# First attention takes one batch's rows through DRAM ahead of its main block, and five stages end with a square root on ScalarE

## The reference, cut to what matters

```python
def _layernorm(x, axis=-1, eps=1e-05):
    m = jnp.mean(x, axis=axis, keepdims=True)
    v = jnp.var(x, axis=axis, keepdims=True)
    return (x - m) / jnp.sqrt(v + eps)
...
xn = _layernorm(x, axis=-1)
x = x + _L0_attn_ref(xn, ...) + _L0_ffn_ref(xn, ...)
xn = _layernorm(x, axis=-1)
x = x + _L1_attn_ref(xn, ...) + _L1_ffn_ref(xn, ...)
...
```

```python
q = (x @ Wq + bq).reshape(b, h, dh, t)
k = (x @ Wk + bk).reshape(b, h, dh, t)
v = (x @ Wv + bv).reshape(b, h, dh, t)
attn = jnp.einsum('bhdt,bhds->bhts', k, v) * temperature
attn = jax.nn.softmax(attn, axis=-1)
out = jnp.einsum('bhdt,bhts->bhds', q, attn)
```

## Time and profile before

| | |
|---|---|
| runs, median (lowest to highest) | 2434.83 us (2428.15 to 2442.73), 3 runs |
| profiled execution, its time | 2452.63 us |
| its span in the trace | 2451.0 us |
| mean granted TensorE clock | 0.884 |
| PE busy | 2014.1 us (82%) |
| DVE busy | 1738.9 us (71%) |
| ACT busy | 1195.2 us (49%) |
| POOL busy | 536.9 us (22%) |

### The profile page before, as it was taken

How to read it: one execution, slowest core, us unless ns; L and a number is a source line. 1 busy time by engine, 2 the same in 40 slices (tenths; PEclk the granted TensorE clock), 3 DMA queues, 4 the chain that set the end, 5 groups by cost and what they waited for, 6 DMA issues and landing times. The chain is left out here.

```text
span 2451.0 us, 45364 instructions
## 1 busy us (share of the span) xinstructions
PE 2014.1 (82%) x17632; PEld 1041.8 (43%) x17632; DVE 1738.9 (71%) x2865; ACT 1195.2 (49%) x2429; POOL 536.9 (22%) x640
## 2 busy tenths in 40 slices
PE   1788876965739999899789879988799798797898
PEld 1222222632302339633343248845544345555554
DVE  3899998667789885598554963355666697866665
ACT  2899998233408772488533223324443021075433
POOL 1112110014954431244402521125300000001100
PEclk8798999976659999899877889978899899988899
DMA  7423420001723226333100122201123423000000
GB/s 253 80 53 80 77 53 1 1 17 45 193 79 102 51 53 202 82 70 46 19 10 16 38 69 89 94 28 36 44 66 92 155 77 98 5 6 25 1 0 35
DMA packets 146772, 155.89 MB, mean 64 GB/s; under 512 B 53004, under 2 KB 122314, under 8 KB 146562
## 3 DMA queue, kind: packets, MB, share of 16 engines
q1 hardware_dynamic: 131912, 119.78, 18.9%
q0 software_dynamic: 12928, 25.47, 4.0%
q10 hardware_dynamic: 1728, 7.87, 0.8%
HBM read 87.37 MB, written 68.55 MB: 64 GB/s over the span
## 5 line engine op out<-in xcount | busy, mean ns | idle before, releaser
L427 ACT ACTIVATE a_E<-a_scores,a_nmax 128x512 f32<-128x512 f32 x512 | 343.6, 816 | 11.7 <-DVE a_nmax L360 11.4
L999 ACT ACTIVATE a_E<-a_scores 128x512 f32<-128x512 f32 x512 | 272.8, 601 | 115.5 <-PE a_scores L1032 105.2
L902 DVE TENSOR_REDUCE a_nmax<-a_first 128x2 f32<-128x1024 f32 x256 | 297.0, 1218 | 27.4 <-PE a_first L1022 25.1
L360 DVE TENSOR_REDUCE a_nmax<-a_scores 128x2 f32<-128x1024 f32 x256 | 302.6, 1218 | 18.4 <-PE a_scores L442 14.2
L442 PE MATMUL a_scores<-a_Vh,a_Kh 48*128 48x512 bf16 x512 | 107.7, 419 | 100.7 <-ACT a_E L427 71.6
L1032 PE MATMUL a_scores<-a_Qh,a_Kh 51*128 51x512 bf16 x512 | 165.8, 397 | 18.9 <-PEq L50 6.5
L455 PE MATMUL a_turn<-a_E,a_QS 128*32 128x256 f32 x2048 | 174.8, 418 | 2.4 <-DVE a_QS L370 2.1
L1022 PE MATMUL a_first<-a_Kh,a_Qh 48*128 48x512 bf16 x512 | 148.1, 421 | 29.5 <-DVE a_nmax L902 15.8
L427 ACT ACTIVATION_READ_ACCUMULATOR a_E<-a_scores,a_nmax 128x1 f32 x512 | 167.4, 336 | 0.0
L1054 PE MATMUL a_out<-a_E,a_V 128*32 128x256 f32 x2048 | 162.7, 398 | 0.5 <-ACT a_E L999 0.5
L442 PEld LDWEIGHTS a_scores<-a_Vh,a_Kh 48*128 48x128 bf16 x512 | 24.9, 94 | 221.5 <-ACT a_E L427 180.6
(11 more groups left out here) (482 smaller groups left out, 4543.7 us busy)
## 6 DMA issues: line engine op xcount, KB each, us to landing
f_up<-in_L_up SPq DMA_DIRECT2D x32, 256.0 KB, 3.4
slots<-zeros ACTq DMA_DIRECT2D x12, 640.0 KB, 15.3
a_Kh<-a_rows_k SPq DMA_DIRECT2D x16, 384.0 KB, 6.8
a_Vh<-a_rows_v SPq DMA_DIRECT2D x16, 384.0 KB, 10.2
a_Qh<-a_rows_q SPq DMA_DIRECT2D x32, 192.0 KB
a_Kh<-a_rows_k SPq DMA_DIRECT2D x32, 192.0 KB
f_xe<-slots SPq DMA_DIRECT2D x40, 128.0 KB, 2.0
outs<-f_ye POOLq DMA_DIRECT2D x40, 128.0 KB
```

Source lines behind the costliest of these rows:

```text
L360: v.tensor_reduce(nmax[:, rd % 2, r1, :, q], bank(b, u)[:], AX.X, ALU.max, negate=True).then_inc(S["max_ready"], 1)
L427: m = a.activation(E[:, u % NE, x], bank(b, u)[:, x], ACT.Exp, bias=nmax[:, rd % 2, r1, x, q:q + 1], accum_out=Z[:, rd % 2, r1, x, q:q + 1])
L902: v.tensor_reduce(out, slot_bank(n)[:], AX.X, ALU.max, negate=True).then_inc(S["slot_read"], 1)
L999: a.activation(E[:, u % NE, x], ps_s[n % 3][:], ACT.Exp, scale=SCALE).then_inc(S["exp_ready"], 1)
```

## The change

There are two edits.

**The preamble of the first attention** no longer sends batch 1's rows out and back. SP spills batch 0, waits for it, and issues batch 0's load; then the preamble's block can end. Batch 1's parts are still made there, but into `parts_next`, the buffer of the main block. In the main block SP waits until batch 0's load has landed, spills batch 1, waits, loads batch 1, and goes on with batch 2 as before. POOL now waits for the spill of the batch before also for its first use of `parts_next` (batch 2).

**A square root of one column** (`g.unit_root`, 128 x 1) is put at the end of ScalarE's list in five blocks: the first (ahead of ln0), f0 (ahead of ln1), the last attention block of L1 (ahead of ln2), the last block of L2 (ahead of ln3), and the block of f3 between ln3a and ln3b. Its result is used by nobody.

```diff
@@ attention0, preamble
-            parts = k1.sb("a0_parts", [128, FIRST, 3, 2 * T], BF16)
+            parts = [k1.sb("a0_parts", [128, 3, 2 * T], BF16), parts_next]
...
                 def _(sp):
-                    for b in range(FIRST):
-                        sp.wait_ge(S["parts_ready"], b + 1)
-                        spill_left(sp, rows_k[b], parts[:, b, :, 0:T], spilled[b])
-                        spill_right(sp, rows_v[b], parts[:, b, :, T:2 * T], spilled[b])
-                    for b in range(FIRST):
-                        sp.wait_ge(spilled[b], NSP)
-                        load(sp, b, b)
+                    sp.wait_ge(S["parts_ready"], 1)
+                    spill_left(sp, rows_k[0], parts[0][:, :, 0:T], spilled)
+                    spill_right(sp, rows_v[0], parts[0][:, :, T:2 * T], spilled)
+                    sp.wait_ge(spilled, NSP)
+                    load(sp, 0, 0)
@@ attention0, main block
             def _(sp):
-                for b in range(FIRST, NB):
+                sp.wait_ge(rows_sem[0], 64)
+                for b in range(1, NB):
                     n = b - FIRST + 1
-                    sp.wait_ge(S["parts_ready"], n)
+                    if n > 0:
+                        sp.wait_ge(S["parts_ready"], n)
                     spill_left(sp, rows_k[b], parts[:, :, 0:T], S["spilled"])
                     spill_right(sp, rows_v[b], parts[:, :, T:2 * T], S["spilled"])
-                    sp.wait_ge(S["spilled"], n * NSP)
-                    sp.wait_ge(S["scores_ready"], (b - 1) * NU)
+                    sp.wait_ge(S["spilled"], b * NSP)
+                    if n > 0:
+                        sp.wait_ge(S["scores_ready"], (b - 1) * NU)
                     load(sp, b, b % 2)
...
                     pool.wait_ge(S["kv_ready"], n)
-                    if n > 1:
-                        pool.wait_ge(S["spilled"], (n - 1) * NSP)
+                    pool.wait_ge(S["spilled"], n * NSP)
@@ f0, at the end of ScalarE's list (the same line ends it in L2's last block and in f3's block ahead of ln3b)
+                a.activation(g.unit_root[:], g.ident[:, 0:1], ACT.Sqrt)
@@ L1's attention
                 copy_out(m_last)
+                if m_last == NMH - 1:
+                    a.activation(g.unit_root[:], g.ident[:, 0:1], ACT.Sqrt)
@@ build, the first block
+        g.unit_root = g.sb("unit_root", [128, 1])
...
+                a.activation(g.unit_root[:], zeros[:, 0:1], ACT.Sqrt)
```

More of the change, by code:

```diff
@@ L198, in attention0 @@
         temp_bk = k.sb("a0_temp_bk", [128, C])
+        parts_next = k.sb("a0_parts_next", [128, 3, 2 * T], BF16)
         c1 = ExitStack()
@@ L208, in attention0 @@
                 "parts_ready")}
-            spilled = [g.sem(f"a0p_spilled{i}") for i in range(FIRST)]
+            spilled = g.sem("a0p_spilled")
             with nc.Block() as block:
@@ L247, in second @@
                         v.wait_ge(S["first_cast"], b + 1)
-                        v.tensor_tensor(rest[:, s], KV[:, s], parts[:, b, 0], ALU.subtract).then_inc(S["second_rest"], 1)
+                        v.tensor_tensor(rest[:, s], KV[:, s], parts[b][:, 0], ALU.subtract).then_inc(S["second_rest"], 1)
                     def third(b):
@@ L252, in third @@
                         v.wait_ge(S["second_cast"], b + 1)
-                        v.tensor_tensor(rest[:, s], rest[:, s], parts[:, b, 1], ALU.subtract).then_inc(S["third_rest"], 1)
+                        v.tensor_tensor(rest[:, s], rest[:, s], parts[b][:, 1], ALU.subtract).then_inc(S["third_rest"], 1)
                     v.wait_ge(g.a0_loaded, 7 * 16)
@@ L267, in first @@
                         a.wait_ge(S["kv_ready"], b + 1)
-                        a.copy(parts[:, b, 0], KV[:, b % 2]).then_inc(S["first_cast"], 1)
+                        a.copy(parts[b][:, 0], KV[:, b % 2]).then_inc(S["first_cast"], 1)
                     a.wait_ge(g.a0_loaded, 7 * 16)
@@ L277, in _ @@
                         a.wait_ge(S["second_rest"], b + 1)
-                        a.copy(parts[:, b, 1], rest[:, s]).then_inc(S["second_cast"], 1)
+                        a.copy(parts[b][:, 1], rest[:, s]).then_inc(S["second_cast"], 1)
                         if b + 1 < FIRST:
@@ L285, in _ @@
                         pool.wait_ge(S["third_rest"], b + 1)
-                        pool.tensor_copy(parts[:, b, 2], rest[:, b % 2]).then_inc(S["parts_ready"], 1)
+                        pool.tensor_copy(parts[b][:, 2], rest[:, b % 2]).then_inc(S["parts_ready"], 1)
         NU = H0 * R // 2
@@ L296, in attention0 @@
         KV, rest = k.sb("a0_KV_next", [128, 2 * T]), k.sb("a0_rest_next", [128, 2 * T])
-        parts = k.sb("a0_parts_next", [128, 3, 2 * T], BF16)
+        parts = parts_next
         S = {n: g.sem(f"a0_{n}") for n in (
```

## The result

The changed kernel takes 2422.24 us in the median of 20 runs (2416.42 to 2445.38), the kernel before 2434.18 in 20 beside it (2427.16 to 2445.55). The ratio is 0.9959, 95% interval 0.9944 to 0.9974: faster by 0.41%, 10.0 us, between 6.3 and 13.6. The two medians lie 11.9 us apart, which is inside that interval. I had forecast 7.1 us and 2427.7, within 2417 to 2437.

What follows compares the result with a forecast made beforehand. ScalarE's exponentials pace the first attention's main block, but the edits touch stretches of waiting, the preamble's bound by DMA bytes in queue order. 4.16 + 0.05 + 2.9 = 7.1 us off 2434.8 gives 2427.7 us, range 2417 to 2437.

Steps and rivals of the forecast that it cites:

- Layer norms 1, 2, 3, 3b: Table load moved ahead of the barrier saves 1.04 us at each of four layer norms, 4.16 us, at no cost.
- Layer norm 0: First block: the load also moves, but the projections wait for the last weight, so gain 0.05 us, bounds 0 and 1.04.
- The preamble: First attention: batch 0's load is issued near 48.9, first scores come at 61.1, 2.9 us earlier; bounds 2.0 and 4.3.
- the way: First attention's preamble: time from the first spill's issue to the first scores, 18.8 us by the forecast.
- 1.03 us after the last byte: Preamble: delay from a spill's last byte to the queue's release, putting batch 0's release at 48.9; lower bound 0.3.
- Cover of batch 1's rows: First attention: batch 1's load ends near 80, its scores are due at 105.3; 25 us of cover, cost 0.
- Sum: Whole kernel: 4.16 + 0.05 + 2.9 = 7.1 us faster, 2427.7 us; bounds 6.2 and 9.5.
- 1: Rival: only the layer norms gain, batch 0's load being bound by something else; gain 4.2 us, 2430.6; chance 0.08.
- 2: Rival: at the layer norms the root's cover is gone or the moved load saves nothing; gain 2.9 us; chance 0.05.
- 4: Rival: an unseen drain of 1.28 us stood ahead of each layer norm load; sum 12.2 us, 2422.6; chance 0.07.
- 3, the clock: Rival: TensorE's half clock lasts some 30 us longer in TensorE-bound stretches, costing 15 us, 2442.7; chance 0.10.

Runs made afterwards that it cites:

- the double load: The change plus an unused one-column exponential in each layer norm's ScalarE list, so each makes two table loads; ratio 1.0041 to the kernel before.
- the filled gap: The change plus eight transposes on TensorE ahead of its wait for the first attention's weights; ratio 0.9958 to the kernel before.
- the longer one: The change with the temperature's DMA issued last, behind three feed-forward weights, so the projections wait longer; ratio 0.9964 to the kernel before.
- without the wait: The change without SP's wait for batch 0's load, so batch 1's spill is queued right behind that load; ratio 0.9979 to the kernel before.
- the repetition: The changed kernel as it is, measured again beside the kernel before; ratio 0.9946, median 2445.49 us against 2454.74.
- The parts alone: Two kernels against the kernel before: only the preamble's edit without added roots, and only the five roots with the old preamble; ratio 0.9987 each.

## Why the prediction was right, and where it was off

**Layer norms 1, 2, 3, 3b: 4.16 us, right.** Each is 0.47 to 0.48 us from variance to reciprocal where it was 1.51 to 1.52, in every profile with the roots but that of the double load. Two loads and a small activation put 3.02 us between variance and reciprocal. By the Trainium skill, "ScalarE: Activation LUTs", section "What ACT_TABLE_LOAD costs", a load takes 1283 ns, which agrees with the 1.28 us here, and a drain of about 1380 ns comes with each switch; by that an estimate for the two is 3.02 + 2 x 1.38 = 5.8 us. No row here shows such a drain, and the measurement decides. That the added roots are free in these places is shown by the rows too: the smallest cover left is 3.3 us.

**Layer norm 0: 0.05 us forecast, 0.0 measured.** The step was right: 10.92 us from its variance to the projections against 10.95 before, and 9.91 where the weights come early. What the prediction left out is a consequence, which it didn't count: the microsecond saved becomes idle time of TensorE, 2.55 us instead of 1.55, and behind such a gap its clock was found at half (1.2 GHz) in two profiles of three. That costs 1.6 to 2.6 us at the projections. The gap as the cause is supported by the ten profiles of ten at full clock behind shorter gaps, and by the filled gap and the longer one, which came out as it says. It isn't proven: these two have one profile each, one of the three at 2.55 us was at full clock too, and the share of executions that it hits isn't known.

**The preamble: 2.9 us forecast, 4.2 measured.** This is the mis-sized term. Over the eleven profiles with the edit the way is 16.65 to 17.8 us, mean 17.4; over the three without it 21.6, 21.3 and 21.7. My sum made it 18.8. Of the 1.4 us too much, 0.6 was in "1.03 us after the last byte": in the change the spill's bytes move from 46.0 to 50.6 and the queue goes on at 51.11, half a microsecond behind. In the kernel before, the last byte at 52.53 was my sum and no row, at a time when batch 0's load was in the queue too. The other 0.8 was the load, forecast at 12.2 us from its issue to the scores and 11.4 in the mean of the eleven: I had put its bytes at 153 GB/s, 10.3 us, and in the change they took 9.0 us at 174, from 52 to 61 us.

The 153 was a poor rate for two reasons. Its window, 54 to 72 us, leaves out the head of the load, and a load starts quicker: in the change 216 and 201 GB/s in its first two microseconds. And rates vary. Over 6 us of each load, some 2 to 3 us behind its first bytes, they are 155, 164 and 163 GB/s in the three profiles of the old preamble and 161 to 177 in ten of the new one; in the eleventh, without the wait, it is 183, where bytes of the spill behind it may be counted too. So the profile that I forecast from had the slowest load of all, and whether the other load behind it costs anything, these numbers don't show: in the kernel before, the rate stayed at 154 GB/s from 66 to 72 us, when batch 0's load had landed.

**Cover of batch 1's rows: right.** They were on the chip by 80 us, the loads of batches 2 to 7 are issued 44.2 to 45.0 us apart, and no wait of TensorE for them shows.

**Sum.** 4.2 + 4.16 + 0 is 8.4 us, less the clock at the projections in those executions that it hits. Measured were 10.0 us (6.3 to 13.6), and in the repetition 13.3 (8.1 to 18.4). The point is above my count both times, the intervals reach it. The parts alone, 3.2 us each, and the change without the first root, 5.4, point the other way. Over the six kernels that hold both edits with the zeros where they were (the change twice, without the first root, without the wait, gap filled, gap longer) the gains are 10.0, 13.3, 5.4, 5.1, 10.3 and 8.8 us, in the mean 8.8. So nothing over the 8.4 us needs a cause. That the forecast of 7.1 came so near had some luck in it: the preamble gave 1.3 us more than I counted, and the clock, which I hadn't counted there, took 1.6 to 2.6 away in some executions.

**The rivals.** 1 is out: the load came earlier and the time from spill to scores got shorter by 4.2 us. 2 is out by the rows. 4 is out by the double load. 3, the clock, was the right kind of thing to name but in the wrong place: not some long stretch far behind, but short ones right behind a wait. Besides the projections there is batch 0 of the attention: from the first scores to GpSimd's first work it took 30.7 us in the first profile before, where the clock rose late, and 28.1 to 30.4 elsewhere; and f0, 71.7 us from the attention's last addition to ln1 where its first matmuls ran at half clock, 69.0 in the change's profile where they ran at full, 70.7 mostly. Between the first pair of profiles they give 2.1 and 2.6 us, a little more than the whole 4.3 between first scores and ln1. I see no tie to the edits: the second profile of the change has 70.76 for f0, and so has the second of the kernel before.

## What to carry to other kernels

A table load ahead of a barrier is free only as far as ScalarE idles there, and worth only what the first user behind the barrier waited for: read both from the idle times in the timeline, here 1.04 of the 1.28 us. Where a layout goes through DRAM and back, let only what is needed first stand in the queue; and ask what the bulk transfers at the start delay. Here zeros in buffers that no other instruction touched before 716 us held back the input and cost as much as the whole change gained. A microsecond saved in front of a wait for a transfer is more idle time for TensorE, and here its clock was at half behind that wait in two profiles of three.

Two profiles of the same kernel differed by 18 us in one stage, and two of the kernel before by 6% in the rate of one load. Differences between profiles should be read within a stretch that begins and ends at marks of the same chain, and checked in a second profile, before they are put down to a change.

## What I had not expected of the hardware

TensorE's clock after short idle time: behind gaps of up to 2.0 us it was at full (2.4 GHz) in ten profiles of ten, behind 2.54 to 2.56 us at half (1.2 GHz) in two of three, behind 4.31 us in the one tried. At half, eight projections of 128 columns took 2.08 us instead of 1.13.

The transfers by kind: spills (rows of SBUF to DRAM) ran at 340 GB/s, loads of the same 1.57 MB (DRAM to 48 partitions at a time) at 153 to 174, with the DMA engines' share at 1.00 for the spills and 1.05 to 1.15 for the loads. The share alone doesn't show that a load moves half as much.
